# First feed-forward: the last six chunks of rounded weights divided between GpSimd and VectorE, in another order

## The chip, the cores and the metric

The kernel runs on one core of one Trainium2 chip. The metric is the device time of one execution in microseconds, the median of several. In all texts PE is the matrix engine (TensorE), DVE is VectorE, ACT is ScalarE, POOL is GpSimd and SP is SyncE, the engine that issues most loads. Each engine takes its instructions in the order in which they are written, and waits at one until the semaphores it names have reached their counts.

## What is computed

Two transformer layers on `x` (32 x 64 rows of 256 features), each a cross-attention and a feed-forward with residuals. The change lies in the first feed-forward. Its weights are rounded to e4m3 first, and everything else is computed in float32:

```python
def _quantized_matmul(x, w, scale):
    wq = w.astype(jnp.float8_e4m3fn).astype(x.dtype)
    y = jnp.einsum('bsi,io->bso', x, wq)
    return y * scale
gate = jax.nn.silu(_quantized_matmul(x, gate_w, gate_scale))
up = _quantized_matmul(x, up_w, up_scale)
fuse = gate * up
return _quantized_matmul(fuse, down_w, down_scale)

x = x + _L0_xattn_ref(_layernorm(x, axis=-1), ctx_1024, ...)
x = x + _L0_ffn_ref(_layernorm(x, axis=-1), ...)
```

The rows are 2048, the hidden width is 768.

## The kernel before

The rows lie on 128 partitions as 16 tiles (`NT`). Every engine has one program, written out by hand, and no scheduler changes it: an instruction's place in its engine's program is its order. The stages follow each other and overlap at their ends: first attention (to about 160 us), first feed-forward (about 158 to 245 us), second attention in 64 units (to about 650 us), second feed-forward.

**The first feed-forward** works through 24 steps u = 6 g + j: four groups g of 512 rows (`NG`), and in each six blocks j of 128 hidden features (`J0`). A step is `gate(u)` and `up(u)` on PE (four matmuls of 512 columns each, since the rows are split into a high part `xT_hi` and a low part `xT_lo`), `silu_of(u)` on ACT, `hidden(u)` on DVE (the product, `hid`), `hidden_hi(u)` on ACT and `hidden_lo(u)` on POOL (the two parts of `hid`), and `down(g, j)` on PE (eight matmuls), which adds the block into the group's output. PE runs two steps behind itself: behind `gate(u)` and `up(u)` stands `down` of step u - 2. The first steps are mixed with the end of the attention: `gate(0)` to `up(3)` stand between the last transposes and outputs, and `down(0, 0)` waits for `rows_updated(15)`, which adds the attention's last output to x (it frees the bank, semaphore `x_updated`). On ACT `silu_of(u)` stands ahead of `hidden_hi(u - 1)`. The helper `hidden_hi(u)` and `hidden_lo(u)` also wait for `down` of step u - 2, because there are two buffers.

**The rounding of the weights** (`w0`). They lie in `w0_raw` as 18 chunks of 256 columns. Chunks 0 to 11 are gate and up weights, chunk 12 + j is the block j of the down weights. A chunk takes four operations: `w0_magic` on DVE (lines 458 and 460, the power of two times a constant, in one of the two buffers of `rnd`), and `w0_rounded` on POOL (line 421 adds it to `w0_raw`, line 423 subtracts it again and writes `w0`). Each of the last two counts `w0_steps` up by one, and chunk n + 1 begins only in turn behind chunk n. `down` waits in the first group:

```python
if g == 0:
    pe.wait_ge(w0_steps, 2 * (2 * KD * PER_J + j + 1))
```

that is for chunk 12 + j. The last five chunks (from `W0_LATE` = 13) are rounded during the feed-forward: chunk 13 behind `hidden_lo(1)`, chunk 12 + u behind `hidden_lo(u)` for u = 2 to 5.

**Beside it** ACT and POOL split the weights of the next attention, a chunk of 256 columns in each step: `weights_hi(u)` on ACT and `weights_lo(u)` on POOL (line 664, `w_lo` in the trace), which stands ahead of `hidden_lo(u)`. `normal(t, ...)` on DVE (line 803) normalises a tile of rows, `rows_updated(t)` is lines 817 to 819 and 468, and `roots` on POOL (lines 475 and 477) takes the inverse roots for the normalisation.

Of the kernel before, what the change touches and what calls it, by code (L numbers as in the profile page):

```python
# [21 lines left out]
ALU = mybir.AluOpType  # L22
# [6 lines left out]
NT = ROWS // P  # L29
# [19 lines left out]
J0 = I0 // P  # L49
GT = 4  # L50
GR = GT * P
NG = NT // GT
# [20 lines left out]
W0_CHUNKS = W0_COLS // W_CHUNK  # L73
PER_J = I0 // W_CHUNK
W0_ORDER = [PER_J * n + c for c in range(PER_J) for n in range(2 * KD)] + list(range(2 * KD * PER_J, W0_CHUNKS))
W0_STEPS = (2, 3, 4, 5, 6, 8, 9, 10, 12, 13, 14)
W0_LATE = W0_CHUNKS - 5
W_PIECE = 1024
W_PIECES = W1_COLS // W_PIECE
NU = NP * NS  # L80
# [17 lines left out]
def after(eng, sem, count):  # L98

    if isinstance(count, int) and count <= 0:  # L100
        return
    eng.wait_ge(sem, count)
# [16 lines left out]
def run_groups(steps, step, first=0):  # L119


    for u in range(first, NG * steps):
        step(*divmod(u, steps), u % 2)
# [7 lines left out]
def build(nc, A, out):  # L131
# [6 lines left out]
    with root:  # L138
        def sb(stack, name, shape, dt=F32):
            return stack.enter_context(nc.sbuf_tensor(name, shape, dt))  # L140

        def sem(name):
            return root.enter_context(nc.semaphore(name))
# [19 lines left out]
        rnd = sb(root, "rnd", [P, 2, W_CHUNK])  # L163
# [13 lines left out]
        w0_raw = sb(sr, "w0_raw", [P, W0_COLS])  # L177
# [21 lines left out]
        w0 = sb(s0, "w0", [P, W0_COLS], F32R)  # L199
# [137 lines left out]
        magic_steps, w0_steps = sem("magic_steps"), sem("w0_steps")  # L337
# [56 lines left out]
        def y_bank(t):  # L394

            return bank[2 if t < NT - 2 else 4]
# [9 lines left out]
        def w0_part(n):  # L406

            c = W0_ORDER[n]
            return slice(c * W_CHUNK, (c + 1) * W_CHUNK)

        def w0_magic(dve, n):

            if n == 0:
                dve.wait_ge(w0_in, 3 * 16)
            after(dve, w0_steps, 2 * (n - 1))
            e4m3_magic(dve, magic_steps, 2 * n, w0_raw[:, w0_part(n)], rnd[:, n % 2, :])

        def w0_rounded(pool, n):

            pool.wait_ge(magic_steps, 2 * n + 2)  # L420
            pool.tensor_tensor(w0_raw[:, w0_part(n)], w0_raw[:, w0_part(n)], rnd[:, n % 2, :], ALU.add).then_inc(w0_steps, 1)
            pool.wait_ge(w0_steps, 2 * n + 1)
            pool.tensor_tensor(w0[:, w0_part(n)], w0_raw[:, w0_part(n)], rnd[:, n % 2, :], ALU.subtract).then_inc(w0_steps, 1)

        def third_order_step(pool, base, y, half, tmp, low):

            pool.tensor_tensor(tmp, y, y, ALU.mult).then_inc(newton, 1)
            pool.wait_ge(newton, base + 1)
            pool.tensor_tensor(tmp, tmp, half, ALU.mult).then_inc(newton, 1)
            pool.wait_ge(newton, base + 2)  # L430
            pool.tensor_scalar(low, tmp, -5.0 / 3.0, None, ALU.add).then_inc(newton, 1)
            pool.wait_ge(newton, base + 3)
            pool.tensor_tensor(tmp, tmp, low, ALU.mult).then_inc(newton, 1)
            pool.wait_ge(newton, base + 4)
            pool.tensor_scalar(tmp, tmp, 1.25, None, ALU.add).then_inc(newton, 1)
            pool.wait_ge(newton, base + 5)
            pool.tensor_tensor(y, y, tmp, ALU.mult).then_inc(newton, 1)
# [11 lines left out]
        def weights_in(eng, g, j):  # L449

            u, chunks = J0 * g + j, W_PIECE // W_CHUNK
            if u % chunks == 0:
                eng.wait_ge(piece_in[u // chunks], 16)

        def e4m3_magic(eng, done, base, w, magic):


            eng.tensor_scalar(magic.bitcast(U32), w.bitcast(U32), 0x7F800000, None, ALU.bitwise_and).then_inc(done, 1)
            eng.wait_ge(done, base + 1)
            eng.tensor_scalar(magic, magic, E4M3_LEAST, 1.5 * 2.0 ** 20, ALU.max, ALU.mult).then_inc(done, 1)  # L460
# [144 lines left out]
        def _(pool):  # L605
# [30 lines left out]
            def step(i, k):  # L636
# [17 lines left out]
                if i in (7, 11):  # L654
                    roots(pool, 1, i - 7)
            run_steps(A_FIRST, A_LAST, step)


            def weights_lo(u):

                cols = bass.ds(u * W_CHUNK, W_CHUNK)
                weights_in(pool, *divmod(u, J0))
                pool.wait_ge(w1_hi_ready, u + 1)
                pool.tensor_tensor(w1_lo[:, cols], w1_raw[:, cols], w1_hi[:, cols].bitcast(F32), ALU.subtract).then_inc(w1_lo_ready, 1)

            def hidden_lo(u):

                par = u % 2
                pool.wait_ge(hid_hi_ready, u + 1)
                after(pool, down_done, u - 1)  # L670
                pool.tensor_tensor(hid_lo[:, par, :], hid[:, par, :], hid_hi[:, par, :].bitcast(F32), ALU.subtract).then_inc(hid_lo_ready, 1)  # L671
# [2 lines left out]
            roots(pool, 1, NT - 2 * GT)  # L674
            w0_rounded(pool, 11)
            probabilities0(NT - 1)
            w0_rounded(pool, 12)
            rows_biased(NT - 1)
            hidden_lo(0)
            weights_lo(0)  # L680
            hidden_lo(1)
            w0_rounded(pool, W0_LATE)
            weights_lo(1)

            def step(g, j, par):
                u = J0 * g + j
                if j == 4 and g > 0:
                    roots(pool, 2, GT * (g - 1))
                if u == 4:
                    roots(pool, 1, NT - GT)  # L690
                weights_lo(u)
                hidden_lo(u)
                if u <= W0_CHUNKS - W0_LATE:
                    w0_rounded(pool, W0_LATE + u - 1)
            run_groups(J0, step, 2)


            def differences(u, roots_of):
# [68 lines left out]
        def _(dve):  # L767
# [45 lines left out]
            def rows_updated(t):  # L813

                dve.wait_ge(y_done, t + 1)
                dve.wait_ge(x_biased, t + 1)
                dve.tensor_tensor(x_sb[:, t, :], y_bank(t)[:, 0:D], x_sb[:, t, :], ALU.add).then_inc(x_updated, 1)
                dve.wait_ge(x_updated, t + 1)
                dve.bn_stats(row_bn[:, t, :], x_sb[:, t, :]).then_inc(row_steps, 1)
                moments(dve, 1, t, 1)  # L820
# [80 lines left out]
            def hidden(u):  # L901

                j, par = u % J0, u % 2
                dve.wait_ge(up_done, u + 1)
                dve.wait_ge(silu_ready, u + 1)
                after(dve, hid_lo_ready, u - 1)
                dve.scalar_tensor_tensor(hid[:, par, :], bank[2 + par][:, :], up_sc[:, j:j + 1], silu[:, par, :],
                                         ALU.mult, ALU.mult).then_inc(hid_ready, 1)
# [2 lines left out]
                lo_of(n, bank[n], fT_hi, fT_lo)  # L911
            differences0(NT - 1)
            w0_magic(dve, 11)
            w0_magic(dve, 12)
            exponential_sums0(NT - 1)
            hidden(0)
            for r in range(GT, 2 * GT):
                normal(r, f_xhat, f_xhat_ready, fT_done)
            hidden(1)
            w0_magic(dve, W0_LATE)  # L920
            rows_updated(NT - 2)

            def step(g, j, par):
                u = J0 * g + j
                hidden(u)
                if u == 2:
                    rows_updated(NT - 1)
                if j == 0 and 0 < g < NG - 1:
                    for r in range(GT):
                        normal(GT * (g + 1) + r, f_xhat, f_xhat_ready, fT_done)  # L930
                if j == 1 and g > 0:
                    group_scaled(g - 1)
                if j == 2 and g > 0:
                    group_output(g - 1)
                if j in (1, 2) and g > 1:
                    lo_of(2 * (g - 2) + j - 1, bank[6 + (j - 1)], cxT_hi, cxT_lo)
                if j == 3 and g > 0:
                    group_stats(g - 1)
                if j == 3 and g == NG - 1:
                    ctx_lo(0, 0)  # L940
                if j == 4 and g == NG - 1:
                    dve.wait_ge(g_in, 2 * 16)
                    dve.tensor_tensor(gk_q[:, :], gq_gk[:, 0:1], gq_gk[:, 1:2], ALU.mult).then_inc(g_ready, 1)
                if j in (3, 4) and g < NG - 1:
                    lo_of(2 * (g + 1) + j - 3, bank[6 + (j + 1) % 2], fT_hi, fT_lo)
                if j == 4 and g > 0:
                    moments(dve, 2, GT * (g - 1), GT)
                if u <= W0_CHUNKS - W0_LATE:
                    w0_magic(dve, W0_LATE + u - 1)
                if j == 5 and g > 0:  # L950
                    for r in range(GT):
                        normal(GT * (g - 1) + r, c_xhat, c_xhat_ready, cxT_done)
# [16 lines left out]
            def group_stats(g):  # L969

                for b in range(2):
                    dve.wait_ge(f_updated, 2 * g + b + 1)
                    for r in range(2):
                        t = GT * g + 2 * b + r
                        dve.bn_stats(row_bn[:, t, :], x_sb[:, t, :]).then_inc(row_steps, 1)
            run_groups(J0, step, 2)

            def fold_lo(n):
                dve.wait_ge(m_hi_ready, n + 1)
# [955 lines left out]
```

## Time and profile before

| what | value |
|---|---|
| median of 3 runs | 722.06 us (721.88 to 723.37) |
| the profiled execution | 722.73 us |
| its span, first to last instruction | 720.9 us |
| PE busy | 660.1 us (92%) |
| DVE busy | 548.9 us (76%) |
| ACT busy | 479.7 us (67%) |
| POOL busy | 436.0 us (60%) |
| mean granted clock of PE | 0.99 |

Times inside the trace count from the start of the span. "Granted clock" is the share of PE's full clock (2.4 GHz) that the chip let it have; 0.50 is 1.2 GHz. Busy time is an average over all stages: which engine ends a wait has to be read in the stage itself.

### The profile page before, as it was taken

To read this page: it belongs to the slowest core of one execution; us is meant where nothing else is said; L and a number is where in the kernel's file an instruction comes from. 1 tells how busy PE (TensorE), PEld (TensorE's weight loads), DVE (VectorE), ACT (ScalarE), POOL (GpSimd) and SP (SyncE) were. 2 spreads that over 40 slices of the span, in tenths; PEclk is the share of its full clock that TensorE was granted. 3 is DMA by queue.
4 is the path that set the end of the run, shared out by engine and by line. 5 is a ranking of instruction groups with operands and counts; after the bars stand their busy time and mean duration, and the time that the engine had idled before them with its cause. 6 is when DMAs were issued, how large, how long until landed. Compare 5 with 4: busy or idle time off the path is not lost.

```text
span 720.9 us, 16231 instructions
## 1 busy us (share of the span) xinstructions
PE 660.1 (92%) x5782; PEld 527.8 (73%) x5782; DVE 548.9 (76%) x1180; ACT 479.7 (67%) x982; POOL 436.0 (60%) x618
## 2 busy tenths in 40 slices
PE   2789999988899999999999999999999999999784
PEld 1567777667788877888888888888888888876442
DVE  3699999999787877676777676676767766766887
ACT  1577877756466576666666666666666666658994
POOL 2378878878877545565656656665656554464500
PEclk9999999999999999999999999999999999999997
DMA  8200003203201000000000100000100000000001
GB/s 282 77 9 9 10 9 117 70 1 106 86 1 38 15 1 2 15 30 9 23 24 17 28 9 25 23 16 16 31 9 16 15 1 3 1 1 1 31 29 60
DMA packets 26019, 22.83 MB, mean 32 GB/s; under 512 B 5041, under 2 KB 24402, under 8 KB 25810
## 3 DMA queue, kind: packets, MB, share of 16 engines
q1 hardware_dynamic: 24160, 20.92, 9.2%
q8 instruction: 47, 0.77, 0.5%
q10 hardware_dynamic: 1778, 0.86, 0.4%
q14 instruction: 34, 0.28, 0.1%
HBM read 19.67 MB, written 2.10 MB: 30 GB/s over the span
## 4 chain that ended last, share of the span: by engine, by line
POOL 38%; issue 26%; PE 15%; DVE 14%; ACT 3%; ACTq 1%; POOLq 1%; DVEq 0%
POOL rstd L734 14%; POOL pr L702 5%; POOL p_n L709 5%; PE banks L1594 2%; POOL w L725 2%; POOL w_raw L722 2%; PE banks L1613 2%; PE banks L1614 2%; DVE h_sum L1093 2%; DVE hid_b L1086 2%; POOL var L732 1%; POOL qk_norm L644 1%; DVE h_magic_b L1091 1%; DVE half L852 1%; POOL hid_lo L671 1%
## 5 line engine op out<-in xcount | busy, mean ns | idle before, releaser
L734 POOL TENSOR_TENSOR rstd<-var,minus_half 128x8 f32<-128x8 f32 x64 | 106.1, 1657 | 5.0
L709 POOL TENSOR_TENSOR p_n<-pr,pinv 128x256 f32<-128x256 f32 x64 | 39.3, 614 | 75.7 <-DVE pinv L1001 75.7
L702 POOL TENSOR_TENSOR pr<-pr,rstd 128x256 f32<-128x256 f32 x63 | 38.6, 613 | 74.1 <-DVE pr L1011 74.0
L1316 ACT ACTIVATE kT<-banks,gk_q 128x512 f32<-128x512 f32 x64 | 44.0, 688 | 49.1 <-PE banks L1755 49.1
L1745 PE MATMUL banks<-m_hi,z_hi 128*128 128x256 f32 x256 | 74.9, 293 | 0.7 <-DVE z_lo L992 0.6
L1745 PE MATMUL banks<-m_hi,z_lo 128*128 128x256 f32 x256 | 72.3, 283 | 0.0
L1745 PE MATMUL banks<-m_lo,z_hi 128*128 128x256 f32 x256 | 72.3, 282 | 0.0
L992 DVE TENSOR_TENSOR z_lo<-banks,z_hi 128x512 fp32r<-128x512 f32 x64 | 43.9, 686 | 29.1 <-ACT z_hi L1301 29.0
L1039 DVE TENSOR_REDUCE sums<-q_sq 128x4 f32<-128x512 f32 x64 | 43.7, 683 | 25.2 <-ACT q_sq L1340 25.2
L1362 ACT ACTIVATE qT<-banks 128x512 f32<-128x512 f32 x64 | 38.2, 597 | 32.9 <-PE banks L1849 32.9
L1007 DVE TENSOR_REDUCE pmax<-banks 128x4 f32<-128x256 f32 x64 | 27.0, 422 | 41.1 <-PE banks L1776 41.0
L1336 ACT ACTIVATE q_rows<-banks 128x512 f32<-128x512 f32 x64 | 38.2, 598 | 29.0 <-PE banks L1441 28.9
L1745 PEld LDWEIGHTS banks<-m_hi,z_hi 128*128 128x128 f32 x256 | 48.6, 190 | 9.6 <-DVE z_lo L992 7.5
L1439 PE MATMUL banks<-w_hi,xT_hi 128*128 128x512 f32 x128 | 50.4, 393 | 0.0
L1441 PE MATMUL banks<-w_hi,xT_lo 128*128 128x512 f32 x128 | 50.0, 390 | 0.0
L1440 PE MATMUL banks<-w_lo,xT_hi 128*128 128x512 f32 x128 | 49.9, 390 | 0.0
L1745 PEld LDWEIGHTS banks<-m_lo,z_hi 128*128 128x128 f32 x256 | 48.8, 190 | 1.0
L1301 ACT ACTIVATE z_hi<-banks 128x512 fp32r<-128x512 f32 x64 | 38.1, 595 | 16.9 <-PE banks L1793 15.8
L1745 PEld LDWEIGHTS banks<-m_hi,z_lo 128*128 128x128 f32 x256 | 48.7, 190 | 0.0
L1776 PE MATMUL banks<-kT,qT 128*64 128x64 f32 x1024 | 43.9, 228 | 0.8 <-DVE pr L1011 0.4
L1849 PE MATMUL banks<-ident,q_rows 128*128 128x128 f32 x256 | 40.5, 281 | 3.5 <-ACT kT L1316 1.8
L1058 DVE TENSOR_TENSOR k_sc<-banks,rstd 128x512 f32<-128x512 f32 x64 | 43.6, 681 | 0.1
(194 smaller groups left out, 2059.2 us busy)
## 6 DMA issues: line engine op xcount, KB each, us to landing
w_raw<-in_L_xattn_Wq SPq DMA_DIRECT2D x4, 512.0 KB, 5.8
wo_raw<-in_L_xattn_Wo SPq DMA_DIRECT2D x1, 2048.0 KB, 9.2
k_ctx<-in_ctx SPq DMA_DIRECT2D x16, 128.0 KB, 2.7
w_raw<-in_L_ffn_w_gating SPq DMA_DIRECT2D x16, 128.0 KB, 2.3
out_x<-x_sb SPq DMA_DIRECT2D x4, 512.0 KB, 2.9
x_sb<-in_x SPq DMA_DIRECT2D x1, 1536.0 KB, 9.3
a_ctx<-in_ctx SPq DMA_DIRECT2D x16, 64.0 KB, 1.8
w_raw<-in_L_xattn_Wk SPq DMA_DIRECT2D x2, 512.0 KB, 9.1
```

The costliest lines, as they stand in the source:

```text
L702: pool.tensor_tensor(pr[:, u % 2, :, :], pr[:, u % 2, :, :], roots_of[:, HC:2 * HC].unsqueeze(2).to_broadcast([P, HC, S]), ALU.mult).then_ ...
L709: pool.tensor_tensor(p_n[:, u % 2, :, :], pr[:, u % 2, :, :], pinv[:, u % 2, :].unsqueeze(2).to_broadcast([P, HC, S]), ALU.mult).then_inc( ...
L734: pool.tensor_tensor(rstd1[:, par, :], var1[:, :], minus_half[:, :].to_broadcast([P, 2 * HC]), ALU.pow).then_inc(root1, 1)
L992: dve.tensor_tensor(z_lo[:, w % 2, :, :].rearrange("p c n -> p (c n)"), bank[4 + w % 2][:, :], z_hi[:, w % 2, :, :].bitcast(F32).rearrange ...
L1039: dve.tensor_reduce(sums[:, 1 - par, HC:2 * HC], q_sq[:, :, :], AX.X, ALU.add).then_inc(q_sum_ready, 1)
L1058: dve.tensor_tensor(k_sc[:, par, :, :], k_bank[par][:, :].rearrange("p (h n) -> p h n", n=DH), rstd1[:, par, 0:HC].unsqueeze(2).to_broadca ...
L1316: act.activation(kT[u % 2][:, :, :].rearrange("p h n -> p (h n)"), bank[2][:, :], ACT.Copy, scale=gk_q[:, :]).then_inc(kT_ready, 1)
L1439: nc.tensor.matmul(out_, wh, vh, start=start, stop=False)
L1440: nc.tensor.matmul(out_, wh, vl, start=False, stop=False)
L1441: return nc.tensor.matmul(out_, wl, vh, start=False, stop=stop)
L1745: last = nc.tensor.matmul(bank[6][:, za * D:(za + 1) * D], z[:, odd, c, :], mm[:, h, :], start=w % NS == 0 and c == 0 and m == 0, stop=w % ...
L1776: last = nc.tensor.matmul(bank[3][q, n * S:(n + 1) * S], qT[:, u % 2, n, q], kT[u % 2][:, n, q], start=True, stop=True)
```

## The change

Six chunks are now late (`W0_LATE` = 12). Of them 12, 14 and 16 are done as before, by DVE and POOL together; 13, 15 and 17 are done by DVE alone, with all four operations (`w0_rounded_here`). On POOL chunk 12 stands behind `weights_lo(0)`, chunk 14 behind `hidden_lo(3)` and chunk 16 behind `hidden_lo(5)`. On DVE `hidden(1)` and the magic of chunk 12 stand ahead of four `normal`, `hidden(2)` is taken out of the loop, and chunk 13 and then `rows_updated(15)` follow it. The last `weights_lo` stands behind the last `hidden_lo`. PE's, ACT's and SP's programs are the same as before.

```diff
-W0_LATE = W0_CHUNKS - 5
+W0_LATE = W0_CHUNKS - 6
...
+        def w0_rounded_here(dve, n):
+
+            w0_magic(dve, n)
+            dve.wait_ge(magic_steps, 2 * n + 2)
+            dve.wait_ge(w0_steps, 2 * n)
+            dve.tensor_tensor(w0_raw[:, w0_part(n)], w0_raw[:, w0_part(n)], rnd[:, n % 2, :], ALU.add).then_inc(w0_steps, 1)
+            dve.wait_ge(w0_steps, 2 * n + 1)
+            dve.tensor_tensor(w0[:, w0_part(n)], w0_raw[:, w0_part(n)], rnd[:, n % 2, :], ALU.subtract).then_inc(w0_steps, 1)
...
             probabilities0(NT - 1)
-            w0_rounded(pool, 12)
             rows_biased(NT - 1)
             hidden_lo(0)
             weights_lo(0)
+            w0_rounded(pool, W0_LATE)
             hidden_lo(1)
-            w0_rounded(pool, W0_LATE)
             weights_lo(1)
...
-                weights_lo(u)
+                if u < NG * J0 - 1:
+                    weights_lo(u)
                 hidden_lo(u)
-                if u <= W0_CHUNKS - W0_LATE:
+                if u in (3, 5):
                     w0_rounded(pool, W0_LATE + u - 1)
             run_groups(J0, step, 2)
+            weights_lo(NG * J0 - 1)
...
             w0_magic(dve, 11)
-            w0_magic(dve, 12)
             exponential_sums0(NT - 1)
             hidden(0)
+            hidden(1)
+            w0_magic(dve, W0_LATE)
             for r in range(GT, 2 * GT):
                 normal(r, f_xhat, f_xhat_ready, fT_done)
-            hidden(1)
-            w0_magic(dve, W0_LATE)
             rows_updated(NT - 2)
+            hidden(2)
+            w0_rounded_here(dve, W0_LATE + 1)
+            rows_updated(NT - 1)
...
                 hidden(u)
-                if u == 2:
-                    rows_updated(NT - 1)
...
                 if u <= W0_CHUNKS - W0_LATE:
-                    w0_magic(dve, W0_LATE + u - 1)
+                    (w0_magic if u % 2 else w0_rounded_here)(dve, W0_LATE + u - 1)
...
-            run_groups(J0, step, 2)
+            run_groups(J0, step, 3)
```

**POOL, from `hidden_lo(2)` on.** Before (`hid_lo` is `hidden_lo`, `w1_lo` is `weights_lo`, the two lines with `rnd` are a chunk; the semaphores that a row waits for stand in brackets):

```order
L671 TENSOR_TENSOR hid_lo<-hid,hid_hi 128x512 [waits down_done,hid_hi_ready]
L421 TENSOR_TENSOR w0_raw<-w0_raw,rnd 128x256 [waits magic_steps]
L423 TENSOR_TENSOR w0<-w0_raw,rnd 128x256 [waits w0_steps]
L664 TENSOR_TENSOR w1_lo<-w1_raw,w1_hi 128x256 [waits w1_hi_ready]
L671 TENSOR_TENSOR hid_lo<-hid,hid_hi 128x512 [waits down_done,hid_hi_ready]
L421 TENSOR_TENSOR w0_raw<-w0_raw,rnd 128x256 [waits magic_steps]
L423 TENSOR_TENSOR w0<-w0_raw,rnd 128x256 [waits w0_steps]
```

and now:

```order
L680 TENSOR_TENSOR hid_lo<-hid,hid_hi 128x512 [waits down_done,hid_hi_ready]
L673 TENSOR_TENSOR w1_lo<-w1_raw,w1_hi 128x256 [waits w1_hi_ready]
L680 TENSOR_TENSOR hid_lo<-hid,hid_hi 128x512 [waits down_done,hid_hi_ready]
L421 TENSOR_TENSOR w0_raw<-w0_raw,rnd 128x256 [waits magic_steps]
L423 TENSOR_TENSOR w0<-w0_raw,rnd 128x256 [waits w0_steps]
```

The first chunk behind `hidden_lo(2)` was chunk 14; it now comes one `w1_lo` and one `hid_lo` later, and chunk 15 is gone from POOL.

**DVE, from `hidden(1)` on.** Before (line 907 is `hidden`, 817 to 468 are `rows_updated`, 458 and 460 the magic of a chunk):

```order
L907 SCALAR_TENSOR_TENSOR hid<-banks,up_sc,silu 128x512 [waits silu_ready,up_done]
L458 TENSOR_SCALAR rnd<-w0_raw 128x256 [waits w0_steps]
L460 TENSOR_SCALAR rnd<-rnd 128x256 [waits magic_steps]
L817 TENSOR_TENSOR x_sb<-banks,x_sb 128x256 [waits x_biased,y_done]
L819 BN_STATS row_bn<-x_sb 128x6 [waits x_updated]
L468 BN_AGGR row_stats<-row_bn 128x2 [waits row_steps]
L907 SCALAR_TENSOR_TENSOR hid<-banks,up_sc,silu 128x512 [waits hid_lo_ready,silu_ready,up_done]
L817 TENSOR_TENSOR x_sb<-banks,x_sb 128x256 [waits x_biased,y_done]
```

and now, from the `rows_updated(14)` that stands behind the four `normal`:

```order
L827 TENSOR_TENSOR x_sb<-banks,x_sb 128x256 [waits x_biased,y_done]
L829 BN_STATS row_bn<-x_sb 128x6 [waits x_updated]
L477 BN_AGGR row_stats<-row_bn 128x2 [waits row_steps]
L917 SCALAR_TENSOR_TENSOR hid<-banks,up_sc,silu 128x512 [waits hid_lo_ready,silu_ready,up_done]
L467 TENSOR_SCALAR rnd<-w0_raw 128x256 [waits w0_steps]
L469 TENSOR_SCALAR rnd<-rnd 128x256 [waits magic_steps]
L430 TENSOR_TENSOR w0_raw<-w0_raw,rnd 128x256 [waits w0_steps,magic_steps]
L432 TENSOR_TENSOR w0<-w0_raw,rnd 128x256 [waits w0_steps]
L827 TENSOR_TENSOR x_sb<-banks,x_sb 128x256 [waits x_biased,y_done]
```

Between `hidden(2)` and the last `rows_updated` now stand the four operations of chunk 13; before, nothing stood there.

## Rows read from the trace of the kernel before

**Rows 1.** The page, part 4: the chain that ended last, by engine.

```profile
POOL 38%; issue 26%; PE 15%; DVE 14%; ACT 3%; ACTq 1%; POOLq 1%; DVEq 0%
```

**Rows 2.** Timeline of PE: start, us, line, operation [idle before <-releaser].

```profile
173.96 0.35 PE L1594 MATMUL banks<-w,hid_hi 128*128 128x256 f32 x1 [0.61 <-DVE x_sb L817]
...
176.74 0.48 PE L1613 MATMUL banks<-xT_hi,w 128*128 128x512 f32 x1
...
182.46 0.36 PE L1594 MATMUL banks<-w,hid_hi 128*128 128x256 f32 x1 [0.47 <-POOL w L423]
...
183.49 0.40 PE L1613 MATMUL banks<-xT_hi,w 128*128 128x512 f32 x1
...
187.16 0.36 PE L1594 MATMUL banks<-w,hid_hi 128*128 128x256 f32 x1 [1.67 <-POOL w L423]
...
190.76 0.36 PE L1594 MATMUL banks<-w,hid_hi 128*128 128x256 f32 x1 [0.58 <-POOL w L423]
...
191.78 0.40 PE L1613 MATMUL banks<-xT_hi,w 128*128 128x512 f32 x1
...
201.04 0.40 PE L1613 MATMUL banks<-xT_hi,w 128*128 128x512 f32 x1
...
203.84 0.40 PE L1613 MATMUL banks<-xT_hi,w 128*128 128x512 f32 x1
```

**Rows 3.** Timeline of POOL in the first feed-forward.

```profile
169.16 1.29 POOL L671 TENSOR_TENSOR hid_lo<-hid,hid_hi 128x512 fp32r<-128x512 f32 x1
...
175.96 1.30 POOL L671 TENSOR_TENSOR hid_lo<-hid,hid_hi 128x512 fp32r<-128x512 f32 x1 [0.49 <-ACT hid_hi L1230]
...
187.72 1.34 POOL L671 TENSOR_TENSOR hid_lo<-hid,hid_hi 128x512 fp32r<-128x512 f32 x1
189.02 0.79 POOL L421 TENSOR_TENSOR w_raw<-w_raw,rnd 128x256 f32<-128x256 f32 x1
189.88 0.73 POOL L423 TENSOR_TENSOR w<-w_raw,rnd 128x256 fp32r<-128x256 f32 x1
```

**Rows 4.** Timeline of ACT in the same stretch.

```profile
165.61 0.70 ACT L1241 ACTIVATE silu<-banks,gate_sc 128x512 f32<-128x512 f32 x1
...
175.25 0.63 ACT L1230 ACTIVATE hid_hi<-hid 128x512 fp32r<-128x512 f32 x1 [2.04 <-PE banks L1594]
...
184.62 0.69 ACT L1241 ACTIVATE silu<-banks,gate_sc 128x512 f32<-128x512 f32 x1 [1.99 <-PE banks L1614]
185.20 0.62 ACT L1230 ACTIVATE hid_hi<-hid 128x512 fp32r<-128x512 f32 x1
```

**Rows 5.** Timeline of DVE in the same stretch.

```profile
165.54 3.07 DVE L803 TENSOR_SCALAR f_xhat<-x_sb,row_stats,row_rstd 128x256 f32<-128x256 f32 x4
...
169.19 1.41 DVE L458 TENSOR_SCALAR rnd<-w_raw 128x256 uint32<-128x256 uint32 x1
...
171.27 0.41 DVE L817 TENSOR_TENSOR x_sb<-banks,x_sb 128x256 f32<-128x256 f32 x1
...
173.39 0.42 DVE L817 TENSOR_TENSOR x_sb<-banks,x_sb 128x256 f32<-128x256 f32 x1 [0.35 <-PE banks L1497]
...
182.70 0.28 DVE L458 TENSOR_SCALAR rnd<-w_raw 128x256 uint32<-128x256 uint32 x1
```

**Rows 6.** Line 967: count, least/median/greatest duration in ns, first and last start.

```profile
L967 DVE TENSOR_TENSOR x_sb<-y_tmp,x_sb x8: 678/954/1542, 194.5 to 250.0; 128x512 f32<-128x512 f32 x8
```

**Rows 7.** Timelines of POOL and of PE at the stage's end.

```profile
241.97 0.78 POOL L664 TENSOR_TENSOR w_lo<-w_raw,w_hi 128x256 fp32r<-128x256 f32 x1
242.71 1.32 POOL L671 TENSOR_TENSOR hid_lo<-hid,hid_hi 128x512 fp32r<-128x512 f32 x1
...
244.09 0.39 PE L1594 MATMUL banks<-w,hid_hi 128*128 128x256 f32 x1 [0.69 <-POOL hid_lo L671]
```

**Rows 8.** Windows: us, busy by engine (count), PEclk, DMA share, GB/s.

```profile
149.00:152.00 3.00, 1.23 (x38) 0.83 (x36) 2.97 (x5) 1.67 (x3) 2.50 (x7) 1.00 0.00 0
152.00:157.00 5.00, 4.85 (x28) 3.61 (x29) 4.90 (x11) 2.71 (x7) 2.59 (x5) 0.66 0.02 3
...
184.00:189.00 5.00, 3.33 (x19) 2.64 (x18) 3.34 (x4) 1.51 (x3) 4.92 (x6) 1.00 0.02 3
```

## The prediction

> **What bounds the kernel now.** The page comes first: the chain that ended last is POOL's for 38% of the span and PE's for only 15%, so late releases count more than PE's load [rows 1]. The change touches only the first feed-forward, so the next view is PE's timeline from 174 to 204 us. It shows where this stage loses time. `gate(4)` starts at 176.74 and `gate(8)` at 191.78 [rows 2], four steps in 15.04 us. Later steps without transposes run in 203.84 - 201.04 = 2.80 us [rows 2], so four cost 11.2 us and 3.8 us are lost. The loss stands ahead of `down`: 0.47, 1.67 and 0.58 us of idle released by line 423, the subtract that ends a chunk's rounding [rows 2]; the rest lies in smaller pieces around them. Each `down(0, j)` runs behind `up(j + 2)` and needs two things: `hid_lo` of its own j and chunk 12 + j. POOL's timeline shows why chunks are late: POOL is gapless here, and between two `hid_lo` stand a `w1_lo`, an add and a subtract [rows 3]. So the change goes for a real bound. The question is where its new order puts the chunks.
>
> **What the change costs, part by part.**
>
> *Removed from POOL.* Chunks 13, 15 and 17 leave POOL. A chunk costs it 0.79 + 0.73 us [rows 3], so 4.6 us of POOL work go. In itself this can give back at most the 3.8 us above.
>
> *The order of chunk 14 and 16.* This is the largest term. Before, POOL rounds chunk 14 right behind `hid_lo(2)` and chunk 16 behind `hid_lo(4)`. Now chunk 14 stands behind `hid_lo(3)` and chunk 16 behind `hid_lo(5)`, and POOL takes its work in order. PE has not moved: `down(0, 2)` stands behind `gate(4)` and `up(4)` and needs chunk 14, `down(0, 4)` behind `gate(6)` and `up(6)` and needs chunk 16. But `hid_lo(3)` needs `hid_hi(3)`, and ScalarE issues that behind `silu(4)`, which waits for `gate(4)` to end. So chunk 14 cannot be ready sooner than this chain, counted from the start of `gate(4)`:
> - to the start of silu: 184.62 - 183.49 = 1.13 us (measured at `gate(6)`) [rows 2, 4];
> - silu to `hid_hi`: 185.20 - 184.62 = 0.58 us [rows 4];
> - `hid_hi` to `hid_lo`: 175.96 - 175.25 = 0.71 us [rows 3, 4];
> - `hid_lo` to the add: 189.02 - 187.72 = 1.30 us [rows 3];
> - add to subtract: 189.88 - 189.02 = 0.86 us [rows 3];
> - subtract to `down`: 190.76 - 189.88 = 0.88 us [rows 2, 3].
>
> The sum is 5.46 us; gate and up take PE only about 1.9 of it, so PE stands idle some 3.4 us. `down` to the next gate is 191.78 - 190.76 = 1.02 us, so the step lasts 6.48 us. The same holds for chunk 16 from `gate(6)`. Steps 5 and 7 (chunks 15 and 17) should run at 2.80 us: VectorE needs about 1 us for its add and subtract after POOL's chunk, and PE asks for the result a whole step later. So `gate(4)` to `gate(8)` becomes 2 x 6.48 + 2 x 2.80 = 18.56 us against 15.04: **+3.5 us**. The terms are durations that repeat, so I give this 3.0 to 4.0.
>
> *Chunk 13 on VectorE ahead of the last row update.* Before, `rows_updated(15)` starts as soon as PE delivers and releases `down(0, 0)` at 173.96 [rows 2]. Now `hidden(2)` and the whole rounding of chunk 13 stand in front of it. VectorE's own line: `hidden(0)` ends at 165.54; `hidden(1)` must wait for `silu(1)`, 165.61 + 0.70 = 166.3 [rows 4], and ends at 167.0; then magic of chunk 12 and four normals, which took 2.08 (169.19 to 171.27) and 3.07 us in the old order [rows 5]. So `rows_updated(14)` starts at about 172.2 instead of 171.27; with its 1.02 us and `hidden(2)`'s 0.67, chunk 13 begins near 173.9. The magic pair ran in anything from twice 0.28 to 2.08 us [rows 5]. The add and subtract with two SBUF operands VectorE has not done at 128x256. The nearest row is line 967 at 128x512, 678 to 1542 ns [rows 6]: half the size is about 0.4 us free, and 1.3 us if the same 0.86 of delay is added. Chunk 13 costs 1.4 (0.56 + 2 x 0.4) to 4.7 us (2.08 + 2 x 1.3) by that. I take 1.7, near the low end, because POOL has only two `w1_lo` of 0.74 us to do at that place and then waits for `down(0, 0)` itself. So `rows_updated(15)` starts near 175.6 instead of 173.39: **+2.2 us**, with bounds +1.0 (nothing late before, 1.4) and +5.2. Queued behind it are `hidden(3)`, `down(0, 0)`, and through `hid_hi(2)` all of POOL's next steps.
>
> VectorE's operation of 1.41 us at 169.19 ends at 170.60, just behind POOL's `hid_lo`, which holds from 169.16 to 170.45 [rows 3, 5]; alone it takes 0.28. The Trainium skill (SBUF — State Buffer, "Who interferes with whom") says VectorE's two-port operations, and those with two SBUF inputs against a GpSimd instruction that reads SBUF, block whole until the other has ended. By that rule the add and subtract could cost at most the rest of one POOL instruction each, and with POOL nearly idle there this term stays at about 2 us.
>
> *The last `w1_lo` behind the last `hid_lo`.* At the end of the stage PE waits 0.69 us for `hid_lo(23)`, and a `w1_lo` started at 241.97, 0.74 us ahead of it [rows 7]. Swapped, `hid_lo(23)` ends 0.74 us sooner, and `down` can start when `down(22)` has finished: **-0.7 us** (0 if another wait takes over; what reads that `w1_lo` comes later). The other moved waits (weights_lo against the chunks, roots) lie inside the chain above and are in its sum already.
>
> *Without anything else*: 2.2 + 3.5 - 0.7 = **+5.0 us**. Everything behind this stage is compute that starts from it and shifts with it.
>
> *The clock.* PE now stands idle 3.4 us twice, and about 2 us ahead of `down(0, 0)`. The granted clock fell to 0.66 on average (1.2 GHz for most of it) in 152 to 157 us, after three microseconds with PE busy for 1.23; in 184 to 189, with the idle of 1.67 us and 3.33 busy of 5, it stayed at 1.00 [rows 8]. The new gaps are longer than 1.67 us by far, and leave PE as little work as those three microseconds had, so I expect a spell at 1.2 GHz after each of the two long ones. A spell takes away 5 x (1 - 0.66) = 1.7 us of PE's full-speed work, and PE's gate is on the path in each: **+3.4 us**. Bounds: 0, and 5.1 if the gap ahead of `down(0, 0)` counts as well.
>
> The profiled execution took 722.73 us (span 720.9), 0.67 above the median of 722.06. The sum is a difference, 2.2 + 3.5 - 0.7 + 3.4 = +8.4, or 731.1 for such an execution. For a median I write 722.06 + 8.4 = **730.5 us**.
>
> **The rivals.**
> 1. *The waits come, the clock stays up.* For: in 184 to 189 it did [rows 8]. Against: the idle there was half as long as the new ones. Time: 722.06 + 5.0 = 727.1. Chance 0.2.
> 2. *Three spells.* For: the wait ahead of `down(0, 0)` follows a small one ahead of `outputs0(15)`, which needs `rows_updated(14)`. Time: 730.5 + 1.7 = 732.2. Chance 0.2.
> 3. *Faster: POOL's relief wins.* If `hid_lo(3)` and `hid_lo(5)` were done before `up(4)` and `up(6)`, chunks 14 and 16 would be ready when asked for, and all 3.8 us of loss would go: 2.2 - 3.8 - 0.7 = -2.3, or 719.8. It decides at `hid_hi(3)`: it would have to start ahead of `silu(4)`. ScalarE's order and its waits speak against it. Chance 0.06, mostly for a dependence that I misread.
> 4. *No difference.* The stall of `down(0, 0)` stays at +1.0 and what POOL gains offsets it. It needs the same escape as rival 3 for one of the two chunks. 722 us, chance 0.04.
>
> **How the numbers follow.** The likeliest case, two spells, has 0.5: 730.5 us, by its own terms 729 to 732. A measurement of this kernel tells about 0.2% (1.4 us) from no change. Slower by more than that are the main case and rivals 1 and 2: 0.9; within it rival 4: 0.04; faster rival 3: 0.06. The range reaches from 1.1 us under rival 1 (the wait ahead of `down(0, 0)` at its lower bound) to 1.0 us over rival 2 (the same wait a third of the way to its upper bound): 726.0 to 733.2.
>
> **What would show it.** In the new profile PE should stand idle about 3.3 us ahead of the third and the fifth group of `down` matmuls, released by POOL's subtract, and not at all ahead of the fourth and sixth. POOL's add of chunk 14 should start right behind `hid_lo(3)`. `rows_updated(15)` should start near 175.6, behind VectorE's subtract. `gate(4)` to `gate(8)` should last 18.6 us, more with the clock down. The windows from 176 to 200 us should show granted clocks near 0.5. The last `down` should wait for nothing. I am wrong if those idles are released by something else or absent, or if the part behind 245 us changes its length.

## The result, and the profile after

| | median | executions | ratio to before |
|---|---|---|---|
| before | 722.08 us | 721.88 to 723.37 | |
| after | 731.57 us | 730.15 to 732.84 | 1.0122 [1.0102, 1.0142] |

The change makes the kernel slower by 1.2%; 730.5 us with a range of 726.0 to 733.2 was forecast. The profiled execution took 732.84 us (span 731.0, granted clock 0.98) against 722.73 (720.9, 0.99).

PE's timeline from 176 to 206 us, the rows that answer to [rows 2]; of its `down` groups these are the only ones with a wait ahead:

```profile
177.84 0.35 PE L1604 MATMUL banks<-w,hid_hi 128*128 128x256 f32 x1 [1.97 <-DVE x_sb L827]
...
180.61 0.48 PE L1623 MATMUL banks<-xT_hi,w 128*128 128x512 f32 x1
...
186.04 0.36 PE L1604 MATMUL banks<-w,hid_hi 128*128 128x256 f32 x1 [3.34 <-POOL w L423]
...
196.76 0.55 PE L1604 MATMUL banks<-w,hid_hi 128*128 128x256 f32 x1 [3.35 <-POOL w L423]
...
202.04 0.40 PE L1623 MATMUL banks<-xT_hi,w 128*128 128x512 f32 x1
```

The first, third and fifth `down` wait 1.97, 3.34 and 3.35 us, where before the first, fourth, fifth and sixth waited 0.61, 0.47, 1.67 and 0.58. `gate(4)` to `gate(8)` takes 202.04 - 180.61 = 21.43 us; it took 15.04. POOL's timeline shows what the long waits are for (the rows that answer to [rows 3]):

```profile
183.10 1.27 POOL L680 TENSOR_TENSOR hid_lo<-hid,hid_hi 128x512 fp32r<-128x512 f32 x1 [0.50 <-ACT hid_hi L1240]
184.32 0.77 POOL L421 TENSOR_TENSOR w_raw<-w_raw,rnd 128x256 f32<-128x256 f32 x1
185.17 0.72 POOL L423 TENSOR_TENSOR w<-w_raw,rnd 128x256 fp32r<-128x256 f32 x1
...
190.86 1.29 POOL L680 TENSOR_TENSOR hid_lo<-hid,hid_hi 128x512 fp32r<-128x512 f32 x1 [2.85 <-ACT hid_hi L1240]
```

Chunk 14 follows `hid_lo(3)`, which follows `hid_hi(3)` on ACT, which follows `silu(4)`. POOL, gapless here before, now stands idle itself for 2.85 us: taking work from it bought idle time on POOL, since the order had made PE and POOL wait for each other in turn. ACT's timeline has the two links between (for [rows 4]):

```profile
181.82 0.69 ACT L1251 ACTIVATE silu<-banks,gate_sc 128x512 f32<-128x512 f32 x1
182.40 0.62 ACT L1240 ACTIVATE hid_hi<-hid 128x512 fp32r<-128x512 f32 x1
```

From `gate(4)` at 180.61 the chain runs over 181.82, 182.40, 183.10, 184.32 and 185.17 to `down` at 186.04: 5.43 us, forecast 5.46. DVE's timeline ahead of `down(0, 0)` (for [rows 5]), with POOL's beside it:

```profile
174.35 0.75 DVE L917 SCALAR_TENSOR_TENSOR hid<-banks,up_sc,silu 128x512 f32<-128x512 f32 x1
175.02 0.28 DVE L467 TENSOR_SCALAR rnd<-w_raw 128x256 uint32<-128x256 uint32 x1
175.34 0.70 DVE L469 TENSOR_SCALAR rnd<-rnd 128x256 f32<-128x256 f32 x1
176.07 0.83 DVE L430 TENSOR_TENSOR w_raw<-w_raw,rnd 128x256 f32<-128x256 f32 x1
176.93 0.43 DVE L432 TENSOR_TENSOR w<-w_raw,rnd 128x256 fp32r<-128x256 f32 x1
177.28 0.42 DVE L827 TENSOR_TENSOR x_sb<-banks,x_sb 128x256 f32<-128x256 f32 x1
```

```profile
175.02 1.60 POOL L673 TENSOR_TENSOR w_lo<-w_raw,w_hi 128x256 fp32r<-128x256 f32 x2
```

Chunk 13 holds up `rows_updated(15)` from 175.02 to 177.28, 2.26 us. The windows of the same trace (columns as in [rows 8]) show the clock: 0.57 behind each long wait, where PE was busy for 0.70 and 1.41 of the four microseconds before, and 1.00 behind the wait of 1.97.

```profile
176.00:182.00 6.00, 4.16 (x30) 3.98 (x31) 4.22 (x10) 2.20 (x5) 2.04 (x3) 1.00 0.81 271
182.00:186.00 4.00, 0.70 (x4) 0.23 (x2) 2.48 (x4) 1.32 (x3) 3.42 (x5) 1.00 0.62 185
186.00:190.00 4.00, 3.96 (x15) 3.47 (x16) 0.85 (x2) 0.43 (x1) 1.93 (x3) 0.57 0.00 0
...
192.00:196.00 4.00, 1.41 (x7) 0.82 (x5) 3.56 (x6) 1.51 (x3) 2.99 (x5) 1.00 0.00 0
196.00:200.00 4.00, 3.24 (x12) 2.98 (x13) 2.85 (x6) 0.00 (x0) 1.35 (x2) 0.57 0.02 4
```

At the end of the stage POOL runs the last two `hid_lo` back to back, and the wait of 0.69 us [rows 7] is gone:

```profile
250.91 2.64 POOL L680 TENSOR_TENSOR hid_lo<-hid,hid_hi 128x512 fp32r<-128x512 f32 x2
253.52 0.78 POOL L673 TENSOR_TENSOR w_lo<-w_raw,w_hi 128x256 fp32r<-128x256 f32 x1
```

### The profile page after: what moved, and what is told of

Its sections match the earlier page's. It is cut to its first block, busy times and chain, and to the rows that moved or that the text cites. A ratio compares the mean times of both kernels' runs of the same rounds, so it can differ in the third digit from the quotient of the medians.

```text
span 731.0 us, 16234 instructions
## 1 busy us (share of the span) xinstructions
PE 665.1 (91%) x5782; PEld 532.4 (73%) x5782; DVE 550.5 (75%) x1186; ACT 480.1 (66%) x982; POOL 432.1 (59%) x612
## 4 chain that ended last, share of the span: by engine, by line
POOL 36%; issue 26%; DVE 16%; PE 16%; ACT 3%; ACTq 1%; POOLq 1%; DVEq 0%
POOL rstd L744 14%; POOL pr L712 5%; POOL p_n L719 5%; PE banks L1604 3%; PE banks L1623 3%; PE banks L1624 2%; POOL w L735 2%; POOL w_raw L732 2%; DVE h_sum L1103 2%; DVE hid_b L1096 2%; POOL var L742 1%; DVE half L862 1%; POOL qk_norm L653 1%; DVE h_magic_b L1101 1%; DVE h_pow L1098 1%
```

## The stage in numbers

For every kernel four distances between starts in PE's timeline: from `gate(0)` (the first line 1613 or its equal) to `down(0, 0)`, on to `gate(4)`, on to `gate(8)`, and on to the transposes that follow the last `down`. Beside their sum stands the kernel's ratio with its 95% interval, each against the kernel before on its own chip (722.1, 722.7, 723.0 and 722.6 us there). The runs e1 to e11 are told in the next section.

| kernel | to down(0,0) | to gate(4) | to gate(8) | to the end | sum | median us | ratio |
|---|---|---|---|---|---|---|---|
| before | 14.78 | 2.78 | 15.04 | 53.38 | 85.98 | 722.08 | |
| after | 16.59 | 2.77 | 21.43 | 52.63 | 93.42 | 731.57 | 1.0122 [1.0102, 1.0142] |
| e1_fill | 16.29 | 4.33 | 18.52 | 52.64 | 91.78 | 728.32 | 1.0078 [1.0059, 1.0097] |
| e2_pool_sooner | 16.32 | 4.02 | 16.48 | 52.62 | 89.44 | 728.09 | 1.0076 [1.0054, 1.0097] |
| e3_rows_first | 14.77 | 3.49 | 22.55 | 52.64 | 93.45 | 730.11 | 1.0099 [1.0084, 1.0114] |
| e4_before_swap | 15.07 | 2.78 | 15.09 | 52.62 | 85.56 | 723.08 | 1.0001 [0.9987, 1.0016] |
| e7_both | 14.77 | 3.49 | 16.24 | 54.21 | 88.71 | 725.87 | 1.0034 [1.0022, 1.0047] |
| e8_fill_rows | 15.05 | 3.49 | 18.52 | 52.64 | 89.70 | 727.22 | 1.0048 [1.0034, 1.0063] |
| e11_17_sooner | 14.74 | 3.49 | 13.01 | 54.22 | 85.46 | 722.76 | 0.9994 [0.9982, 1.0006] |
| e5_only15 | 14.73 | 2.77 | 14.14 | 52.65 | 84.29 | 721.19 | 0.9972 [0.9960, 0.9984] |
| e6_15_17 | 15.07 | 2.77 | 13.39 | 54.28 | 85.51 | 722.01 | 0.9988 [0.9977, 0.9999] |
| e9_15_noswap | 15.21 | 2.78 | 14.15 | 53.36 | 85.50 | 721.78 | 0.9984 [0.9972, 0.9996] |
| e10_split_later | 14.75 | 2.78 | 13.67 | 52.64 | 83.84 | 720.76 | 0.9973 [0.9960, 0.9987] |

The first distance holds a trap. In every trace but e5's the clock is low for a while somewhere from 150 to 166 us, whatever the order of the chunks. Before, and in e1, e2, e3, e7, e10 and e11, it lies ahead of `gate(0)`; after the change, and in e4, e6, e8 and e9, it lies behind it and adds 0.3 to 0.5 us (15.05 to 15.21 against 14.73 to 14.78). The window of the trace after the change:

```profile
162.00:166.00 4.00, 4.00 (x13) 3.05 (x13) 3.34 (x8) 2.23 (x2) 3.81 (x6) 0.57 0.00 0
```

So of the changed kernel's 1.81 us about 0.3 are this spell. e1 and e2, with the same order on VectorE and the spell ahead of `gate(0)`, have 16.29 and 16.32: the order itself delays `down(0, 0)` by about 1.5 us.

## The experiments

**The clock apart from the waits.** PE does 13 matmuls that nobody reads in each of the two long waits, ahead of `down(0, 2)` and `down(0, 4)`; nothing else differs from the changed kernel. Some 0.4 us of each wait are left.

```diff
 u = J0 * g + j
+if g == 0 and j in (2, 4):
+    pe.wait_ge(fT_lo, 3)
+    for _ in range(13):
+        nc.tensor.matmul(bank[6][:, :], w0_gu[:, 0, 0, 0:P], xT_hi[:, 0, 0:GR], start=True, stop=True)
 pe.wait_ge(hid_lo_ready, u + 1)
```

> The changed kernel with 13 matmuls of 512 columns, whose result nothing reads, put on PE ahead of down(0, 2) and of down(0, 4), where PE stood idle for 3.34 and 3.35 us with the granted clock at 0.50 right after. They take about 3.1 us at full clock, so they should fit into the idle time and delay nothing. Theory (two falls of the clock cost some 3 us of the 9.5): the waits for POOL's subtract shrink to about 0.3 us, the granted clock stays at 1.00 from 178 to 206 us, gate(4) to gate(8) takes 18.5 us instead of 21.4, and the time is about 728.5 us. Rival (the clock is no part of it, the waits alone made the 9.5 us, some of it elsewhere): the stage keeps its 21.4 us and the time stays at 731.5, or gets longer by the matmuls' own 3 us.

Measured 728.32 us (727.65 to 730.38). `gate(4)` to `gate(8)` took 18.52 us with the clock up; the forecast for exactly this was 18.56. So the order costs 18.52 - 15.04 = 3.48 us, and the two spells 21.43 - 18.52 = 2.91 us in the trace, 3.25 between the medians. Here a spell came that the changed kernel's own trace does not have, right behind the wait of `down(0, 0)`:

```profile
175.08 0.36 PE L1608 MATMUL banks<-w,hid_hi 128*128 128x256 f32 x1 [2.16 <-DVE x_sb L827]
...
179.41 0.48 PE L1627 MATMUL banks<-xT_hi,w 128*128 128x512 f32 x1
...
184.90 0.35 PE L1608 MATMUL banks<-w,hid_hi 128*128 128x256 f32 x1 [0.43 <-POOL w L423]
```

```profile
175.00:179.00 4.00, 3.92 (x21) 3.95 (x22) 2.21 (x6) 1.23 (x2) 1.29 (x1) 0.61 1.04 354
```

The first fence is PE's timeline, the second a window of the same trace. The clock is at 0.61 there, and `down(0, 0)` to `gate(4)` takes 4.33 us instead of 2.77. It is a spell at the place where rival 2 has its third; here it is the only one behind `down(0, 0)`, since the two long waits are filled.

**The chunks of POOL one step sooner.** Chunks 14 and 16 stand behind `hidden_lo(2)` and `hidden_lo(4)`.

```diff
-if u in (3, 5):
-    w0_rounded(pool, W0_LATE + u - 1)
+if u in (2, 4):
+    w0_rounded(pool, W0_LATE + u)
```

> The changed kernel with chunk 14 behind hidden_lo(2) and chunk 16 behind hidden_lo(4) on POOL, one step sooner, as in the kernel before; all else as changed. Theory (the place of these two chunks makes the two idles of 3.3 us): the wait ahead of down(0, 2) falls to about 0.7 us and that ahead of down(0, 4) below 1 us. But now chunk 17, on VectorE behind hidden(6) and four normals, becomes the last thing: down(0, 5) should wait some 3 us for it, and down(0, 3) about 1.4 for chunk 15. gate(4) to gate(8) about 17 us plus one fall of the clock, the time about 728 us. Rival (VectorE's extra work makes the loss, wherever POOL does its chunks): the idles ahead of down(0, 2) and down(0, 4) stay, 731.5 us.

Measured 728.09 us. `down(0, 2)` waits no more, `down(0, 3)` waits 0.46 us for chunk 15 where 1.4 were expected, and the stall moves to `down(0, 5)`:

```profile
189.38 0.36 PE L1604 MATMUL banks<-w,hid_hi 128*128 128x256 f32 x1 [0.76 <-POOL w L423]
195.38 0.36 PE L1604 MATMUL banks<-w,hid_hi 128*128 128x256 f32 x1 [2.97 <-DVE w L432]
```

DVE's timeline says why chunk 17 is late. It stands behind `hidden(6)`, which waits for `gate(6)`, and behind four `normal` of 3.12 us:

```profile
188.65 0.75 DVE L917 SCALAR_TENSOR_TENSOR hid<-banks,up_sc,silu 128x512 f32<-128x512 f32 x1 [1.05 <-PE banks L1624]
189.32 3.12 DVE L813 TENSOR_SCALAR f_xhat<-x_sb,row_stats,row_rstd 128x256 f32<-128x256 f32 x4
192.37 0.28 DVE L467 TENSOR_SCALAR rnd<-w_raw 128x256 uint32<-128x256 uint32 x1
192.68 0.29 DVE L469 TENSOR_SCALAR rnd<-rnd 128x256 f32<-128x256 f32 x1
193.01 1.37 DVE L430 TENSOR_TENSOR w_raw<-w_raw,rnd 128x256 f32<-128x256 f32 x1
194.41 0.83 DVE L432 TENSOR_TENSOR w<-w_raw,rnd 128x256 fp32r<-128x256 f32 x1
```

The change had a third place of the same kind, which its two long waits had covered. The one low-clock spell in this stage came behind the wait of 2.16 us ahead of `down(0, 0)`; behind the wait of 2.97 us the clock stayed up:

```profile
196.00:202.00 6.00, 6.00 (x38) 5.32 (x38) 4.41 (x6) 3.32 (x6) 2.26 (x2) 1.00 0.44 168
```

**The row update first.** `rows_updated(15)` stands ahead of chunk 13.

```diff
-w0_rounded_here(dve, W0_LATE + 1)
 rows_updated(NT - 1)
+w0_rounded_here(dve, W0_LATE + 1)
```

> The changed kernel with rows_updated(15) ahead of the rounding of chunk 13 on VectorE instead of behind it. Theory (the four operations of chunk 13 delay the release of down(0, 0)): its wait falls from 1.97 us to under 1, first down 1.3 us sooner against gate(2), chunk 13 is done in time or 0.6 us late for down(0, 1), both idles of 3.3 us stay, and the time is 729.5 to 730.5 us. Rival (the row update is released late by something before it, the chunk lies in VectorE's idle time): nothing changes, 731.5 us.

Measured 730.11 us. `down(0, 0)` comes 16.59 - 14.77 = 1.82 us sooner, of which about 0.3 are the early spell, which lies ahead of `gate(0)` here, and 0.72 us of it go again, because `down(0, 1)` now waits for chunk 13 (0.48 us, released by line 432). The stage's sum is no shorter than after the change, 93.45 us: the first low-clock spell, in the window below, was longer than any after the change, and `gate(4)` to `gate(8)` took 22.55.

```profile
182.00:188.00 6.00, 4.92 (x16) 4.28 (x17) 1.13 (x3) 1.13 (x3) 2.88 (x5) 0.50 0.01 3
```

One trace can't price this part while the clock moves under it, so it was run again with the long waits filled:

> e1_fill (13 idle-filling matmuls ahead of down(0,2) and down(0,4), 728.3 us) with rows_updated(15) ahead of chunk 13 as in e3. It prices the late row update without the low-clock spells of the two long waits. Forecast's term +2.2: 726.1. What e3's trace shows (down(0,0) 1.5 us sooner against its own first gate, 0.7 of it spent again by down(0,1), which then waits for chunk 13 on VectorE): 727.2 to 727.6. The idle ahead of down(0,0) is 0.6 instead of 2.16, and gate(4) to gate(8) lasts 18.5.

Measured 727.22 us (e1 had 728.32), the clock 1.00 from 174 to 198 us, the idle ahead of `down(0, 0)` 0.61, and `gate(4)` to `gate(8)` 18.52. The pairs of traces give the price of the late row update: with the early spell in the same place it delays `down(0, 0)` by 1.5 us (e2 to e7), and `down(0, 1)` takes 0.72 back, so 0.8 us of work order are left; what it adds above that is the chance of a spell. The time fits what was expected by e3's trace (727.2 to 727.6) better than the forecast's +2.2 (726.1), but does not decide by itself: the medians differ by 1.1 us, while the ratios, each against before on its own chip, differ by 0.0030, which is 2.2 us, with overlapping intervals, and e1 may owe part of that to the spell of 1.56 us seen in its trace.

**Both orders put right** (the edits of e2 and e3 together).

> The change with both of its orders put right: rows_updated(15) ahead of chunk 13, and chunks 14 and 16 behind hidden_lo(2) and hidden_lo(4). What stays of the change is the division of the six chunks between the engines and the swap at the end. My theory (two separate terms and what they bring in idle): the two parts add, so 731.6 - 1.5 (row update, as in e3) - 3.5 (order, as in e2) = 726.6 us; down(0,0) idles about 0.6 us, down(0,2) not at all, and down(0,5) still some 3 us, for chunk 17, whose VectorE operations stand behind hidden(6) and so behind gate(6). Rival, the division itself is good and only the orders are bad: no idle over 1 us is left ahead of the first six down groups, and the time is 721 to 722.

Measured 725.87 us, ratio 1.0034: the parts add within their intervals (726.6 expected; the ratios of e2 and e3 add up to 1.0053), and the rival, 721 to 722, fails. `down(0, 5)` still waits 2.98 us for chunk 17, with the clock at 0.60 in the four microseconds behind it. In e2 a wait of the same length had left the clock up.

**Chunk 17 sooner as well**, on DVE ahead of `hidden(6)`.

```diff
-if u <= W0_CHUNKS - W0_LATE:
+if u < W0_CHUNKS - W0_LATE:
     (w0_magic if u % 2 else w0_rounded_here)(dve, W0_LATE + u - 1)
+if u == 5:
+    w0_rounded_here(dve, W0_LATE + 5)
```

> e7_both (both orders put right, 725.9 us) with chunk 17 one step sooner on VectorE, right behind the magic of chunk 16 and ahead of hidden(6). It puts right the third place where the change made a chunk depend on a gate that comes too late. My theory: the 2.98 us of idle ahead of down(0,5) and the low-clock spell that follows it go, gate(4) to gate(8) falls from 16.2 to 13.5 to 14 us, and down(0,1) still waits 0.5 us for chunk 13: 725.9 - 2.4 - 1.6 = 721.9. Rival, VectorE has no room for it: hidden(6) and the output scaling are late, down(1,0) waits some 1.5 to 2 us, and the time is 723.5 or more.

Measured 722.76 us, ratio 0.9994: the loss is gone. Both theories are half right. `gate(4)` to `gate(8)` is the shortest of all, 13.01 us, and the clock stays up; but the rival's wait is there too, 1.36 us ahead of `down(1, 0)`:

```profile
193.07 0.36 PE L1606 MATMUL banks<-w,hid_hi 128*128 128x256 f32 x1 [1.36 <-DVE y_tmp L972]
```

DVE has no room left (e6 below shows the same wait with two chunks), and what it gains ahead of `gate(8)` it gives back right behind it (54.22 us to the end instead of 52.63).

**The swap alone**, in the kernel before.

```diff
-weights_lo(u)
+if u < NG * J0 - 1:
+    weights_lo(u)
 hidden_lo(u)
...
 run_groups(J0, step, 2)
+weights_lo(NG * J0 - 1)
```

> The kernel before with only the last weights_lo put behind the last hidden_lo. Theory: down(23) no longer waits its 0.69 us, and the time is 721.4 us (0.7 less). Rival (the weights' reader or another wait takes its place): 722.1 us.

Measured 723.08 us, ratio 1.0001. In the trace the last part shrinks from 53.38 to 52.62 us and the wait of 0.69 is gone, but the time can't tell 0.7 us from nothing: inconclusive. The pair e5 and e9 below differs by the swap alone and has 0.9972 against 0.9984, 0.9 us, in the direction of the trace and with overlapping intervals.

**How many chunks VectorE can take.** The kernel before with the swap and `w0_rounded_here` for chunk 15 alone, every chunk in its old place:

```diff
-if u <= W0_CHUNKS - W0_LATE:
+if u <= W0_CHUNKS - W0_LATE and W0_LATE + u - 1 not in (15,):
     w0_rounded(pool, W0_LATE + u - 1)
...
-w0_magic(dve, W0_LATE + u - 1)
+(w0_rounded_here if W0_LATE + u - 1 in (15,) else w0_magic)(dve, W0_LATE + u - 1)
```

> The kernel before with the swap at the end and only chunk 15 moved to VectorE, in its old place behind hidden(4). POOL keeps chunks 13, 14, 16 and 17 in the old places and has 1.5 us less to do between hidden_lo(3) and hidden_lo(4), which is where the old waits of 1.67 and 0.58 us came from. My theory (relief helps where the order leaves the chain of hidden_hi alone): gate(4) to gate(8) in 13.5 to 14 us instead of 15.0, and the time 720.2 to 721, ratio 0.998. Rival, a chunk on VectorE delays hidden(5) as much as POOL gains: the stage keeps its 15.0 us and the time is 722 to 722.7.

Measured 721.19 us, ratio 0.9972 [0.9960, 0.9984]: 0.3% faster than the kernel before, clear of the interval, and faster than the changed one. (The old place of chunk 15 on DVE is behind `hidden(3)`, where before its magic stood; the expectation says `hidden(4)`.) PE's timeline has one wait less, and `gate(4)` to `gate(8)` is 14.14 us:

```profile
176.54 0.48 PE L1624 MATMUL banks<-xT_hi,w 128*128 128x512 f32 x1
...
186.12 0.36 PE L1605 MATMUL banks<-w,hid_hi 128*128 128x256 f32 x1 [1.54 <-POOL w L423]
...
189.66 0.36 PE L1605 MATMUL banks<-w,hid_hi 128*128 128x256 f32 x1 [0.51 <-POOL w L423]
...
190.68 0.39 PE L1624 MATMUL banks<-xT_hi,w 128*128 128x512 f32 x1
```

It is 0.1 to 0.6 us over the 13.5 to 14 expected. DVE's subtract cost 1.41 us here beside POOL, and chunk 16 on POOL then waits for DVE's magic. Without the swap:

> e5_only15 (0.9972 of before) without the swap at the end. Theory by the traces: the swap is worth its 0.7 us and chunk 15 on VectorE the other 0.9, so the ratio is 0.9985, some 1.1 us under before. Rival, the swap is worth nothing in the time (as e4 measured): the ratio stays at 0.9972.

Measured 721.78 us, ratio 0.9984 [0.9972, 0.9996], as the traces' theory has it; but the rival's 0.9972 is the end of the interval, so the time alone does not exclude it. With chunk 17 on VectorE as well:

> As e5_only15, with chunk 17 on VectorE too, in its old place behind hidden(6). My theory: gate(4) to gate(8) in about 13 us, but VectorE is then late with the first group's output scaling, and down(1,0) waits about 1.4 us for it, so 720.5 to 721.5, no better than e5. Rival, as in the change, chunk 17 on VectorE stands behind hidden(6) and stops down(0,5) for up to 3 us: 723 to 725.

Measured 722.01 us. `gate(4)` to `gate(8)` falls to 13.39 us, and `down(1, 0)` waits 1.42 us for DVE's scaling of the output, as forecast; the time is 0.5 us over the forecast's end, the stage's sum is 1.2 us longer than e5's, and the second chunk on VectorE is worth nothing. The expectation misnames the place: chunk 17's old place is behind `hidden(5)`, one step sooner than in the change, so this run does not test the rival. It shows that there `down(0, 5)` does not wait for chunk 17 at all. And POOL's splitting later in two steps:

```diff
-if u < NG * J0 - 1:
+if u < NG * J0 - 1 and u not in (4, 5):
     weights_lo(u)
 hidden_lo(u)
...
+if u in (4, 5):
+    weights_lo(u)
```

> e5_only15 with the weights_lo of steps 4 and 5 behind hidden_lo and the chunk instead of ahead of them. In e5 down(0,4) still waits 1.54 us for chunk 16, whose add on POOL follows VectorE's magic by 0.08 us. If POOL's order were the limit, 0.7 us would go: ratio 0.996. My theory: VectorE's magic is now the limit, the wait falls by 0.3 to 0.5 us at most, and the time is within 0.5 us of e5's: ratio 0.9965 to 0.9972.

Measured 720.76 us, ratio 0.9973: within 0.5 us of e5. The wait of `down(0, 4)` fell from 1.54 to 1.07 us, and POOL still stands idle for 0.23 us ahead of its add of chunk 16, until DVE's magic is there, so DVE's magic is the limit. This version and e5 can't be told apart by their ratios; both beat the kernel before and the changed one.

## Why the prediction was right

- *What bounds the stage* and *removed from POOL*: right. POOL's work was the limit (between `hid_lo(3)` and `hid_lo(4)` the reading left out `roots`, 182.27 to 183.57 in the trace before, which is part of it), and relief is worth what the rows said where the order allows it: e5 gains 0.9 us in `gate(4)` to `gate(8)`, e11 2.0 of the possible 3.8.
- *The order of chunks 14 and 16*, +3.5: measured +3.48 (e1 against before). The idles are 3.34 and 3.35 us (3.4), the chain 5.43 (5.46), and the fourth and sixth `down` wait for nothing. Rival 3's escape, `hid_hi(3)` ahead of `silu(4)`, did not occur. Steps 5 and 7 came out right by luck. The forecast's reason was that VectorE needs about 1 us behind POOL's chunk; it left out that chunk 17 stands behind `hidden(6)` and four `normal`. Chunk 17 was in time (done at 198.95, `down(0, 5)` at 201.09) only because the wait of 3.35 us had held PE back; without that wait it is 2.97 us late (e2).
- *Chunk 13*, +2.2: too large. `down(0, 0)` is 1.81 us later against `gate(0)`, and about 0.3 of that are the low-clock spell that before lies ahead of `gate(0)`, so the order made about 1.5. The chunk's four operations held VectorE for 2.26 us (1.7 was taken), but they began sooner than I had it: at 175.02 in a trace whose `gate(0)` is 2.07 us later than before's, so at 172.95 by the old times, where I had 173.9. The two errors partly cancel. As a price of the place it is about 0.8 us only (e2 to e7), since chunk 13 is needed by `down(0, 1)` in any case.
- *The swap*, -0.7: -0.75 in the trace (53.38 to 52.63); in the time not measurable by itself.
- *The clock*, +3.4: two spells, 2.91 us in the traces, 3.25 between the medians: each spell cost about 1.5 us, where 1.7 was taken. Rival 1 is refuted. A spell at the place of rival 2's third occurs in e1 and e2 behind waits of 2.16 us, not in the changed kernel's profiled execution behind 1.97; no trace has all three. That a long wait always brings a spell is not so: it did in all four waits of 3.34 and 3.35 us and behind 2.98 in e7, and did not behind 2.97 in e2.
- *The sum*: 1.81 + 3.48 + 2.91 - 0.75 = 7.45, and the stage's sum grew by 7.44 (the parts are differences of the same distances, so that they add up proves nothing); +8.4 was forecast. The measured ratio is worth 8.8 us (7.4 to 10.3), so the median lies about 1.4 above what this one trace's stage accounts for. In the profiled execution the rest lies outside the stage: 2.07 us ahead of `gate(0)`, where PE ran at a granted clock of 0.74 from 20 to 40 us against 0.91 before, and 0.59 behind the stage. The change touches neither place, and e9, whose programs ahead of `gate(0)` are those of before, has the same 0.74 from 20 to 40 us and its `gate(0)` at 161.17, as late as after the change (161.25; before 159.18). The four executions after the change are 730.15, 730.37, 732.76 and 732.84 us; the median lies between two pairs, and the trace is of the longest. Whether the shorter two lack the early low clock, or a spell in the stage, stays open.

That the median came out within 1.1 us of the forecast is thus partly luck, two errors that cancel: the terms were together 1 us too large, and in the traced execution what lies outside the stage added 2.7 us. The direction, the two long waits and their length are not luck.

## What to carry to other kernels

Moving work off the busiest engine is worth nothing if the new order puts a result that the matrix engine needs behind something that the matrix engine has yet to produce: for every moved step, follow its predecessors on its own engine back to the last thing they wait for, and compare its place with the consumer's. Put each place right and look again, since a stall of 3 us covers the next. An idle of the matrix engine can be paid twice, by its length and by a slower clock behind it, and matmuls without a reader in the gap are a cheap way to measure the two apart.

## What the runs showed of the hardware

- VectorE's add or subtract of two SBUF operands at 128x256 takes 0.42 to 0.43 us alone, and beside POOL's `w_lo` or `hid_lo` it ends 0.28 to 0.29 us after POOL's instruction that it meets. Started at 179.63 in e5 it took 1.41 us, to 181.04, and POOL's `hid_lo` ended at 179.27 + 1.48 = 180.75; after the change 176.07 + 0.83 = 176.90 against 175.02 + 1.60 = 176.62. The two rows of e5:

```profile
179.63 1.41 DVE L432 TENSOR_TENSOR w<-w_raw,rnd 128x256 fp32r<-128x256 f32 x1
```

```profile
179.27 1.48 POOL L680 TENSOR_TENSOR hid_lo<-hid,hid_hi 128x512 fp32r<-128x512 f32 x1
```

  The Trainium skill (SBUF — State Buffer, "Who interferes with whom") has VectorE's second SBUF input come through an interface shared with GpSimd, and calls the sharing an exclusive lock. The rows above agree. One instruction does not: after the change both of chunk 15's operations took 0.43 us while POOL ran a `TENSOR_TENSOR` with two SBUF inputs of 128x4, from 186.13 to 187.30. Why that one holds up nothing no run here shows.

```profile
186.00 0.43 DVE L430 TENSOR_TENSOR w_raw<-w_raw,rnd 128x256 f32<-128x256 f32 x1 [0.75 <-POOL w L423]
186.46 0.43 DVE L432 TENSOR_TENSOR w<-w_raw,rnd 128x256 fp32r<-128x256 f32 x1
```

```profile
186.13 1.17 POOL L486 TENSOR_TENSOR row_rstd<-row_v,minus_half 128x4 f32<-128x4 f32 x1
```

  The add and subtract of a chunk on VectorE therefore cost 0.86 us beside an idle POOL and up to 2.3 beside a busy one (0.87 + 1.41 in e5).
- `hid_lo` on POOL took 1.48 us there and 1.28 to 1.44 us elsewhere in e5. It began at 179.27, before VectorE's add of chunk 15 had ended (178.72 + 0.87 = 179.59), so POOL pays too.
- The clock fell behind a wait of 2.16 us in two kernels and stayed up behind one of 1.97 in a third, and behind one of 2.97 in e2, which is one of the two, so the length of one wait does not tell whether the clock falls. Spells of equal cause differed in length: e3's first lasted about twice as long as the changed kernel's. A single trace of this kernel can be 1.5 to 3 us off by this alone.
